# An adaLN transformer block: the work ahead of the batch loop cut in column chunks and spread over the first batches

## The chip, the cores and the metric

The kernel runs on one core of a Trainium2 chip. The metric is the device time of one launch in microseconds (us), the median of several runs. A core has five engines that run their own instruction streams and meet at semaphores: TensorE (PE, matrix products), VectorE (DVE), ScalarE (ACT), GpSimd (POOL) and SyncE (SP, which here only issues DMA transfers).

## What is computed

For 32 batches of 256 rows by 128 channels:

```python
mod = (silu(c) @ wmod).reshape(32, 6, 1, 128)      # sa, ca, ga, sb, cb, gb
ga, gb = sign(g) * max(|g|, 0.25)                  # both gates
h = layernorm(x) * (1 + ca) + sa
x = x + ga * attention(h, Wq, Wkv, Wo, bo)         # 16 heads of 64, strictly later keys masked
h = layernorm(x) * (1 + cb) + sb
x = x + gb * ffn(h)                                # fp4 block quantiser (blocks of 16) on each input
                                                   # and on w_gate, w_up, w_down; silu(gate) * up
```

All of it is float32. The softmax takes its maximum over all 256 keys and masks afterwards.

## The kernel before

**The loop.** One turn `i` handles batch `i`'s attention, batch `i-1`'s output projection, residual and second layer norm, and batch `i-2`'s feed-forward part, and it prepares batch `i+1` (layer norm, transposed and modulated input). A turn has four stages `j` (PAIRS), each with two units `2j` and `2j+1`; a unit is a pair of heads. `iterations` writes out the turns -1, 0, 1, 2, runs 3 to 30 as a hardware loop, and writes out the last ones. The table `SHARED` is the order, by hand, of what PE writes to the three shared PSUM banks `ps_m` in each stage ("t" transposes of probabilities, "qk" and "v" projections, "xt" the next batch's transposed input, and so on); "qk" of stage `j` serves the units of stage `j+1`.

**How units flow.** PE writes the scores of both units to `ps_s` (`scores`, L922), DVE reduces them to row maxima (`maxima`, L736), PE adds the mask on the diagonal blocks (`mask`, L931), ACT takes exponentials and their sums (`exponentials`, L563), DVE makes reciprocals (`denominators`, L742 and L745), POOL multiplies (`normalize`, L435 and L437), PE transposes (L806), DVE or ACT copies to `probs_t`, PE multiplies with the values (`values`, L949).

**Float32 by parts.** The projections split each float32 operand into a high part (rounded to fp32r) and the rest: ACT writes `wq_r[0]`, `wkv_r[0]` (L512 to L516), DVE subtracts for `wq_r[1]`, `wkv_r[1]` (L611, L617). A product is three matmuls (`matmul_parts`). The transposed input is split in the same way: ACT writes `h_t` and `h_r[0]` (L545), DVE writes `h_r[1]` (L755, with two inputs in SBUF).

**Ahead of turn 0.** SP issues all loads from its one queue, in this order: cond, w_mod, w_q whole, the key half of w_kv, batch 0's x, the value half of w_kv, b_o, w_o, the six pieces of w_gate and w_up, w_down (L370 to L382). ACT makes `tanh` of cond, then the high parts of the three weights of 1024 columns, each as it lands. DVE makes `c_act`, copies `c_t`, writes the low parts of the three weights and `mod_t` (scale and shift of layer norm 1, transposed for all batches) between them; PE transposes `c_act` (L806), multiplies the modulation rows of all batches (L814, two products of 384 columns into `ps_s`) and the two transposed ones (L817). Only then DVE's turn -1 begins: layer norm of batch 0 (`layer_norm_stats` L717, POOL's `rstd` L443 and L445, `normalized` L711), PE's transposes into `ps_m`, ACT's L545, DVE's L755, PE's first two "qk". At the end of turn -1 DVE runs `modulation_rows` (13 steps on 32 x 128 rows, L629 to L641: gates, 1 + cb and so on), which SP stores to `mod_rows` in DRAM for the broadcast loads `mod_a` and `mod_b`, and `weight_scales` (four memsets, L54, L55, L56 of the weight quantiser over 1120 columns). `quantize_magic` of the weights (L62, L65, L66) comes at the end of turn 0, stage 0. POOL runs the three rounding steps (L73, L75, L77) in turn 0, stages 1, 2 and 3. PE transposes the quantised weights in turn 1 at the places `WEIGHT_PLACES` = (0,7), (1,3), (1,4), which later turns use for the feed-forward part; gate of batch 0, at (0,7) of turn 2, is the first to need them.

## Time and profile before

| | before |
|---|---|
| median of 3 runs | 1324.75 us |
| lowest, highest | 1322.56, 1326.55 us |
| the profiled execution: time, span | 1323.2, 1321.3 us |
| busy share PE, DVE, ACT, POOL | 96%, 82%, 63%, 64% |
| mean granted TensorE clock | 0.988 |
| DMA queues, share of 16 engines | 7.0% |

The span is what the profiler saw, from the first instruction to the last; 1.9 us of the run's time lie around it. The busy shares are means over the whole span, so they say little about the opening; for that the windows, the chain and the timeline are read.

### The profile page before, as it was taken

What the parts mean: (1) busy time and instruction counts of PE and PEld (TensorE: products, weight loads), DVE (VectorE), ACT (ScalarE), POOL (GpSimd) and SP (SyncE); (2) the same over time, 40 slices, a digit from 0 to 9 for tenths busy, and PEclk for the clock granted to TensorE, in tenths of its full rate; (3) what the DMA queues carried; (4) which work ended last, traced back from release to release, by engine and by line L of the source; (5) the groups of instructions that cost most, each with busy time, mean ns of one, the idle gap of its engine ahead of it and who ended that gap; (6) DMA issues with size and microseconds to landing.
All of it is one profiled execution on the core that took longest, in us unless ns stands there. A gap on an engine that the chain in (4) does not pass through costs nothing.

```text
span 1321.3 us, 34181 instructions
## 1 busy us (share of the span) xinstructions
PE 1270.0 (96%) x10194; PEld 1033.1 (78%) x10194; DVE 1089.7 (82%) x2565; ACT 837.1 (63%) x2885; POOL 841.2 (64%) x1582
## 2 busy tenths in 40 slices
PE   4999999999999999999999999999999999999984
PEld 3678888788888788888788888888888878888863
DVE  5678888888888888888888888888888888888775
ACT  3666657667667666666766666766666766666640
POOL 1656666766666766666666666676666676666664
PEclk9999999999999999999999999999999999999995
DMA  3000000000000000000000000000000000000000
GB/s 103 18 19 18 12 22 18 22 22 16 12 20 18 22 22 16 20 12 20 20 22 20 17 10 22 18 22 22 16 11 21 18 22 22 16 22 6 19 19 10
DMA packets 38056, 26.53 MB, mean 20 GB/s; under 512 B 2800, under 2 KB 33392, under 8 KB 38032
## 3 DMA queue, kind: packets, MB, share of 16 engines
q1 hardware_dynamic: 38032, 26.23, 7.0%
q8 instruction: 13, 0.21, 0.1%
q14 instruction: 11, 0.09, 0.0%
HBM read 21.94 MB, written 4.28 MB: 20 GB/s over the span
## 4 chain that ended last, share of the span: by engine, by line
PE 92%; DVE 4%; ACT 2%; issue 1%; DMA 1%; POOL 1%; SPq 0%; DVEq 0%; POOLq 0%; ACTq 0%
PE ps_m L827 27%; PE ps_s L922 18%; PE ps_m L806 16%; PE ps_o L949 14%; PE ps_m L873 9%; PE ps_s L931 5%; PE ps_m L897 4%; ACT probs L563 1%; DMA wkv<-L_attn_Wkv 1%; DVE neg_max L736 1%; DVE probs_t L662 0%; DVE qy L62 0%; ACT qk L531 0%; DVE amax L54 0%; DVE qm L66 0%
## 5 line engine op out<-in xcount | busy, mean ns | idle before, releaser
L563 ACT ACTIVATE probs<-ps_s,neg_max 128x128 f32<-128x128 f32 (+1 forms) x1024 | 424.4, 429 | 396.0 <-PE ps_s L931 396.0
L437 POOL TENSOR_SCALAR probs<-probs,r_den 128x256 f32<-128x256 f32 (+1 forms) x768 | 347.6, 468 | 0.0
L736 DVE TENSOR_REDUCE neg_max<-ps_s 128x4 f32<-128x1024 f32 x256 | 303.9, 1218 | 2.5 <-PE ps_s L922 2.3
L922 PE MATMUL ps_s<-qk 64*128 64x256 f32 x2048 | 259.1, 392 | 0.8 <-ACT qk L531 0.8
L662 DVE COPY probs_t<-ps_m 128x512 f32<-128x512 f32 x256 | 176.4, 689 | 80.2 <-PE ps_m L806 76.2
L806 PE MATMUL ps_m<-ident,probs 128*128 128x128 f32 x1536 | 230.9, 273 | 2.4 <-POOL probs L437 1.0
L435 POOL TENSOR_TENSOR probs<-probs,r_den 128x128 f32<-128x128 f32 x256 | 102.1, 399 | 202.5 <-DVE r_den L745 183.8
L922 PEld LDWEIGHTS ps_s<-qk 64*128 64x128 f32 x2048 | 185.3, 187 | 48.3 <-issue 12.3
L563 ACT ACTIVATION_READ_ACCUMULATOR probs<-ps_s,neg_max 128x1 f32 x1024 | 217.7, 213 | 0.0
L73 POOL TENSOR_TENSOR qy<-qy,qm 128x352 f32<-128x352 f32 (+1 forms) x96 | 82.9, 864 | 181.7 <-DVE qm L66 179.4
L949 PE MATMUL ps_o<-probs_t,v 128*64 128x256 f32 (+1 forms) x2048 | 194.7, 332 | 1.5 <-ACT o_t L555 1.5
L949 PEld LDWEIGHTS ps_o<-probs_t,v 128*64 128x64 f32 x2048 | 127.3, 136 | 80.3 <-issue 43.7
L806 PEld LDWEIGHTS ps_m<-ident,probs 128*128 128x128 f32 x1536 | 179.4, 141 | 8.0 <-DVE probs_t L662 2.1
L827 PE MATMUL ps_m<-h_r,wq_r 128*128 128x256 f32 x768 | 156.1, 312 | 2.8 <-DVE h_r L755 2.3
L531 ACT COPY qk<-ps_m 128x512 f32<-128x512 f32 x256 | 153.5, 600 | 3.3 <-PE ps_m L827 3.3
L827 PE MATMUL ps_m<-h_r,wkv_r 128*128 128x256 f32 x768 | 134.1, 283 | 0.0
L873 PE MATMUL ps_m<-wo,o_t 128*128 128x128 f32 x1024 | 121.8, 277 | 0.0
L827 PE MATMUL ps_m<-wkv_r,h_r 128*128 128x512 f32 x384 | 119.0, 418 | 1.4 <-ACT qk L531 1.2
L873 PEld LDWEIGHTS ps_m<-wo,o_t 128*128 128x128 f32 x1024 | 116.8, 192 | 2.9
L827 PEld LDWEIGHTS ps_m<-h_r,wq_r 128*128 128x128 f32 x768 | 108.2, 191 | 11.2 <-DVE h_r L755 2.0
L827 PEld LDWEIGHTS ps_m<-h_r,wkv_r 128*128 128x128 f32 x768 | 110.4, 190 | 0.0
L931 PE MATMUL ps_s<-later_b,ident_b 128*128 128x256 bf16 x512 | 100.9, 279 | 4.0 <-DVE neg_max L736 3.9
(107 smaller groups left out, 1794.2 us busy)
## 6 DMA issues: line engine op xcount, KB each, us to landing
mod_a<-mod_rows SPq DMA_DIRECT2D x32, 256.0 KB, 3.3
x_in<-L_attn_x SPq DMA_DIRECT2D x32, 128.0 KB, 2.1
x_res<-L_attn_x SPq DMA_DIRECT2D x32, 128.0 KB, 2.1
out<-y_out SPq DMA_DIRECT2D x32, 128.0 KB, 1.8
mod_b<-mod_rows SPq DMA_DIRECT2D x32, 64.0 KB, 2.9
wkv<-L_attn_Wkv SPq DMA_DIRECT2D x2, 512.0 KB, 6.9
wq<-L_attn_Wq SPq DMA_DIRECT2D x1, 512.0 KB, 4.1
wo<-L_attn_Wo SPq DMA_DIRECT2D x1, 512.0 KB, 8.2
```

The source lines that it names most:

```text
L435: nc.gpsimd.tensor_tensor(cols, cols, r_den[:, u % 4, 0:1].to_broadcast([P, P]), ALU.mult)
L437: ins = nc.gpsimd.tensor_scalar(cols, cols, r_den[:, u % 4, s:s + 1], 1.0, ALU.mult, ALU.mult)
L531: nc.scalar.copy(qk[:, k % 4, :, :], ps_m[bank][:, :].rearrange("p (n j) -> p n j", n=2)).then_inc(qk_ready, 1)
L563: ins = nc.scalar.activation(probs[:, u % 4, h, t * P:(1 + 2 * t) * P], ps_s[:, 2 * (u % 2) + h, t * N:t * N + (1 + t) * P], ACT.Exp, bias ...
L662: nc.vector.tensor_copy(probs_t[:, 4 * (k % 3):4 * (k % 3) + 4, :], ps_m[bank][:, :].rearrange("p (c j) -> p c j", c=4)).then_inc(pt_ready ...
L736: nc.vector.tensor_reduce(neg_max[:, u % 4, :], ps_s[:, 2 * (u % 2):2 * (u % 2) + 2, :].rearrange("p b (t j) -> p (b t) j", t=2), AX.X, AL ...
L806: return nc.tensor.transpose(dst, src, ident[0:n, 0:n])
L827: mm = nc.tensor.matmul(dst, left[l], right[r], start=(n == 0), stop=(n == 2))
L873: mm = nc.tensor.matmul(ps_m[bank][:, 0:P], o_t[:, u, k * P:(k + 1) * P], wo[:, u, :], start=(u == 0), stop=(u == UNITS - 1))
L922: mm = nc.tensor.matmul(ps_s[:, 2 * (u % 2) + h, t * N:(t + 1) * N], qk[rows, u % 4, 0, t * P:(t + 1) * P], qk[rows, u % 4, 1, :], start=( ...
L931: nc.tensor.matmul(diagonals, ident_b[:, :], later_b[:, :].unsqueeze(1).to_broadcast([P, 2, P]), start=False, stop=True, skip_group_check= ...
L949: mm = nc.tensor.matmul(ps_o[h * DH:(h + 1) * DH, k * N + q0:(k + 1) * N], v[:, keys, col:col + DH], probs_t[:, chunk + 2 * n:chunk + 2 + ...
```

## The change

The body of a turn keeps its order on each engine (it is now written out call by call, with the same sequence); what changes is ahead of turn 0 and in turns 0 and 1. Turn -1 is gone, its work stands ahead of the loop.

- **Loads.** ACT's queue takes batch 0's x and the first 256 columns of w_q. SP's queue takes the rest: w_q and the key half in chunks of 256, 256 and 512 columns, the value half in two of 512, w_mod in one of 256 and one of 512 columns, w_o last of the weights. Batch 1's x is loaded by SP behind all of them.
- **Opening.** DVE clears its padding and normalises batch 0 first. PE makes only the two transposed modulation products before the transposes of batch 0. Only the first chunk's high and low parts lie ahead of the first "qk". Chunk 1 and the first value half follow ahead of turn 0; low parts of chunk 2 and of the second value half are in DVE's turn 0, stage 0; ACT makes their high parts ahead of turn 0.
- **Modulation rows.** PE makes one product of 384 columns in turn 0, stage 0 and one in stage 1, after the scores, into `ps_o`. ACT copies them as its first step of those stages. The 13 steps of row arithmetic run on POOL: 6 before `normalize(0)` of stage 0, 7 in stage 1. SP stores the rows in stage 3 instead of stage 1.
- **Weight quantiser.** DVE takes the maxima at the end of turn 0's stage 0, scales and quotients at the end of stage 1, the two magic steps at the end of stage 2. POOL rounds in turn 0 stage 3, turn 1 stage 0 and turn 1 stage 1. PE's places are (1,7), (2,4), (3,3) of turn 1.

```diff
-        WEIGHT_PLACES = [(0, 7), (1, 3), (1, 4)]
+        WEIGHT_PLACES = [(1, 7), (2, 4), (3, 3)]
+        QK_CHUNKS = (slice(0, 2 * P), slice(2 * P, 4 * P), slice(4 * P, INNER))
+        V_CHUNKS = (slice(INNER, INNER + HALF), slice(INNER + HALF, 2 * INNER))
 # SP
-            sp.dma_start(w_mod_s[:, :], w_mod).then_inc(cond_in, 16)
-            sp.dma_start(wq[:, :], w_q).then_inc(wq_in, 16)
-            sp.dma_start(wkv[:, 0:INNER], w_kv[:, 0:INNER]).then_inc(wk_in, 16)
-            sp.dma_start(x_in[:, :, :], x_v[0]).then_inc(x_loaded, 16)
-            sp.dma_start(wkv[:, INNER:2 * INNER], w_kv[:, INNER:2 * INNER]).then_inc(wv_in, 16)
+            sp.dma_start(w_mod_s[:, 0:2 * P], w_mod[:, 0:2 * P]).then_inc(wmod_in[0], 16)
+            sp.dma_start(wkv[:, QK_CHUNKS[0]], w_kv[:, QK_CHUNKS[0]]).then_inc(wk_in[0], 16)
+            sp.dma_start(wq[:, QK_CHUNKS[1]], w_q[:, QK_CHUNKS[1]]).then_inc(wq_in[1], 16)
+            sp.dma_start(wkv[:, QK_CHUNKS[1]], w_kv[:, QK_CHUNKS[1]]).then_inc(wk_in[1], 16)
+            sp.dma_start(wkv[:, V_CHUNKS[0]], w_kv[:, V_CHUNKS[0]]).then_inc(wv_in[0], 16)
+            sp.dma_start(w_mod_s[:, 2 * P:6 * P], w_mod[:, 2 * P:6 * P]).then_inc(wmod_in[1], 16)
+            sp.dma_start(wq[:, QK_CHUNKS[2]], w_q[:, QK_CHUNKS[2]]).then_inc(wq_in[2], 16)
+            sp.dma_start(wkv[:, QK_CHUNKS[2]], w_kv[:, QK_CHUNKS[2]]).then_inc(wk_in[2], 16)
+            sp.dma_start(wkv[:, V_CHUNKS[1]], w_kv[:, V_CHUNKS[1]]).then_inc(wv_in[1], 16)
...
-                    if i_is(i, 0) and j == 1:
-                        sp.wait_ge(setup_dve, SETUP_ROWS)
+                    if i_is(i, 0) and j == 3:
+                        sp.wait_ge(rows_steps, ROWS_STEPS)
                         sp.dma_start(mod_rows, rows[:, :, :]).then_inc(rows_out, 16)
 # POOL
+            def attention_rows():
+                step = Steps(pool, rows_steps)
+                pool.wait_ge(mod_copied, 1)
+                gate_row(step, 2, 0, 0)
+                pool.wait_ge(bo_in, 16)
+                step(nc.gpsimd.tensor_tensor(rows[:, 1, :], rows[:, 0, :], bo_rows[:, :], ALU.mult))
...
+                    if j == 0:
+                        normalize(i, -1)
+                        if i_is(i, 0):
+                            attention_rows()
+                        if i_is(i, 1):
+                            round_weights(1)
+                        normalize(i, 0)
+                        keep()
+                    elif j == 1:
+                        normalize(i, 1)
+                        if i_is(i, 0):
+                            ffn_rows()
+                        if i_is(i, 1):
+                            round_weights(2)
+                        residual()
+                        input_rstd()
+                        round_hidden(i - 2, 0)
+                        normalize(i, 2)
...
+                    elif j == 3:
+                        normalize(i, 5)
+                        if i_is(i, 0):
+                            round_weights(0)
+                        round_hidden(i - 2, 1)
+                        normalize(i, 6)
+                        round_ffn_in()
+            rstd(0, ln1_pool, ln1_steps, LN_STEPS, mv1, var1, rstd1)
             iterations(pool, body)
 # ACT
-            act.wait_ge(cond_in, 32)
+            act.dma_start(x_in[:, :, :], x_v[0]).then_inc(x_loaded, 16)
+            act.dma_start(wq[:, QK_CHUNKS[0]], w_q[:, QK_CHUNKS[0]]).then_inc(wq_in[0], 16)
+            act.wait_ge(cond_in, 16)
             nc.scalar.activation(c_act[:, :], c_in[:, :], ACT.Tanh, scale=0.5).then_inc(setup_act, 1)
...
+                    if i_is(i, 0) and j < 2:
+                        modulation_copy(j)
...
+            high_parts(0)
+            act.wait_ge(setup_dve, SETUP_MODT)
+            shared = shared_steps(-1)
+            shared_reads(shared, 2, 8)
+            high_parts(1)
+            value_high_part(0)
+            shared_reads(shared, 3, 1)
+            shared_reads(shared, 3, 6)
+            high_parts(2)
+            value_high_part(1)
             iterations(act, body)
 # DVE
+                        maxima(0)
+                        maxima(1)
+                        if i_is(i, 0):
+                            low_parts(2)
...
+                    if i_is(i, 0) and j == 0:
+                        value_low_part(1)
+                        weight_maxima()
+                    if i_is(i, 0) and j == 1:
                         weight_scales()
+                        weight_quotients()
+                    if i_is(i, 0) and j == 2:
+                        weight_exponents()
+                        weight_magic()
...
+            step = Steps(dve, setup_dve)
+            dve.wait_ge(x_loaded, 16)
+            layer_norm_stats(x_in, stats1, mv1, ln1_steps, 0)
+            dve.wait_ge(setup_act, 1)
+            step(nc.vector.scalar_tensor_tensor(c_act[:, :], c_act[:, :], 1.0, c_in[:, :], ALU.add, ALU.mult))
+            step(nc.vector.tensor_scalar(c_act[:, :], c_act[:, :], 0.5, None, ALU.mult))
+            dve.wait_ge(ln1_pool, 2)
+            normalized([xn[:, t, :] for t in range(2)], x_in, mv1, rstd1, xn_ready)
+            dve.wait_ge(setup_pe, 1)
+            step(nc.vector.tensor_copy(c_t[:, :], ps_o[:, 0:B]))
+            dve.wait_ge(setup_pe, 2)
+            step(nc.vector.tensor_copy(mod_t[:, 0, :], ps_o[:, 0:B]))
+            step(nc.vector.tensor_scalar(mod_t[:, 1, :], ps_o[:, B:2 * B], 1.0, None, ALU.add))
+            low_parts(0)
+            dve.wait_ge(ht_ready, 2)
+            nc.vector.tensor_tensor(h_r[1][:, :], h_t[:, :], h_r[0][:, :], ALU.subtract).then_inc(hr_ready, 1)
+            low_parts(1)
+            value_low_part(0)
             iterations(dve, body)
 # PE
+                    if i_is(b, 0) and k in (0, 2, 4):
+                        pe.wait_ge(attn_high, k + 2)
+                        pe.wait_ge(qk_low, k + 2)
...
                     if has.attn:
                         scores(2 * j)
                         scores(2 * j + 1)
+                    if i_is(i, 0) and j < 2:
+                        modulation_matmul(j)
...
+            shared = shared_steps(-1)
+            for place in ((2, 8), (3, 1), (3, 6)):
+                shared_step(*shared[place][0:4])
             iterations(pe, body)
```

## Rows read from the trace of the kernel before

**Rows 1.** Page part 4: shares of the chain that ended last, by engine.
```profile
PE 92%; DVE 4%; ACT 2%; issue 1%; DMA 1%; POOL 1%; SPq 0%; DVEq 0%; POOLq 0%; ACTq 0%
```
**Rows 2.** Windows: stretch, us, busy PE, PEld, DVE, ACT, POOL, clock, DMA, GB/s.
```profile
60.03:97.71 37.68, 36.38 (x298) 28.79 (x296) 26.26 (x63) 24.26 (x86) 17.86 (x38) 1.00 0.06 17
97.71:136.82 39.11, 39.07 (x320) 32.04 (x319) 33.23 (x80) 25.95 (x90) 26.17 (x50) 1.00 0.07 18
126.27:1225.30 1099.03, 1094.38 (x8906) 895.48 (x8904) 936.76 (x2212) 727.56 (x2522) 728.21 (x1372) 1.00 0.07 18
```
**Rows 3.** Chain in order of time, 0 to 62 us: start us, us, what.
```profile
3.07 7.35 DMA wkv<-L_attn_Wkv
...
12.87 0.48 DVE stats L717 x2
...
15.58 0.68 PE ps_m L806 x2
...
17.82 0.47 DVE mod_r L629
...
26.26 0.61 PE ps_s L931 x2
```
**Rows 4.** Timeline of the opening: start us, us, engine line op tiles [idle before].
```profile
0.73 1.28 ACT L509 ACT_TABLE_LOAD   x1 [0.73 <-PEq L983]
...
6.09 2.77 PE L814 MATMUL ps_s<-w_mod_s,c_t 128*32 128x384 f32 x4 [0.36 <-DVE c_t L606]
...
8.79 1.06 PE L817 MATMUL ps_m<-c_t,w_mod_s 128*128 128x32 f32 x4
...
17.39 0.42 DVE L755 TENSOR_TENSOR h_r<-h_t,h_r 128x256 fp32r<-128x256 f32 x1 [1.96 <-ACT h_r L545]
...
17.87 1.01 PE L827 MATMUL ps_m<-h_r,wq_r 128*128 128x256 f32 x3 [1.64 <-DVE h_r L755]
...
20.73 2.69 PE L922 MATMUL ps_s<-qk 64*128 64x256 f32 x16
...
26.70 0.37 ACT L563 ACTIVATE probs<-ps_s,neg_max 128x128 f32<-128x128 f32 x1 [5.28 <-PE ps_s L931]
```
**Rows 5.** Page part 6: DMA issues, KB each, median us from issue to landing.
```profile
x_in<-L_attn_x SPq DMA_DIRECT2D x32, 128.0 KB, 2.1
```
**Rows 6.** Window of PE alone (stretch, us, busy, clock, DMA, GB/s).
```profile
26.00:27.00 1.00, 0.74 (x4) 0.50 0.00 0
```
**Rows 7.** Timeline of PE: the same three matmuls before and after 29 us.
```profile
27.31 0.84 PE L827 MATMUL ps_m<-h_r,wkv_r 128*128 128x256 f32 x3
...
29.73 0.52 PE L827 MATMUL ps_m<-h_r,wkv_r 128*128 128x256 f32 x3
```
**Rows 8.** Page part 5 (busy, mean ns, idle before): a POOL product of 128 columns.
```profile
L435 POOL TENSOR_TENSOR probs<-probs,r_den 128x128 f32<-128x128 f32 x256 | 102.1, 399 | 202.5 <-DVE r_den L745 183.8
```
**Rows 9.** Timeline: POOL's smallest arithmetic step.
```profile
13.80 0.19 POOL L443 TENSOR_TENSOR var<-mv,ln_eps 128x2 f32<-128x2 f32 x1 [10.96 <-DVE mv L721]
```
**Rows 10.** Timeline: POOL normalising beside DVE's weight quotients, and later without them.
```profile
29.28 2.82 POOL L437 TENSOR_SCALAR probs<-probs,r_den 128x256 f32<-128x256 f32 x3
...
29.40 1.53 DVE L62 SCALAR_TENSOR_TENSOR qy_w<-wf,inv_w 128x1120 f32<-128x1120 f32 x1
...
33.58 1.28 POOL L437 TENSOR_SCALAR probs<-probs,r_den 128x256 f32<-128x256 f32 x3
```
**Rows 11.** Timeline of turn 0, stage 2: maxima and the mask behind them.
```profile
40.31 2.55 DVE L736 TENSOR_REDUCE neg_max<-ps_s 128x4 f32<-128x1024 f32 x2
...
42.97 0.11 PEld L931 LDWEIGHTS ps_s<-later_b,ident_b 128*128 128x128 bf16 x2 [0.17 <-DVE neg_max L736]
```
**Rows 12.** Timeline of turn 0, stage 3: a weight rounding step and its neighbours.
```profile
50.72 2.10 POOL L77 TENSOR_TENSOR wfq<-qy_w,scale_w 128x1120 f32<-128x1120 f32 x1
51.00 2.10 DVE L755 TENSOR_TENSOR h_r<-h_t,h_r 128x256 fp32r<-128x256 f32 x1 [0.23 <-ACT h_r L545]
...
53.24 0.59 PE L827 MATMUL ps_m<-h_r,wq_r 128*128 128x256 f32 x3 [0.67 <-DVE h_r L755]
```

More of the change, by code:

```diff
@@ L567, in exponentials @@
                         ins.then_inc(exp_done, 1)
-                    if has.attn:
-                        exponentials(2 * j, 0)
-                        exponentials(2 * j, 1)
-                    first = 5 if j == 2 else 4
-                    for n in range(first):
-                        shared_reads(n)
-                    if has.attn:
-                        exponentials(2 * j + 1, 0)
-                    for n in range(first, 6):
-                        shared_reads(n)
-                    if j == 1 and has.prev:
-                        out_copy()
```

543 lines of the change are left out of this document (354 added, 189 removed).

## The prediction

> **What bounds the kernel now.** I read the chain of the whole span first: 92% of it is PE, 4% DVE, 1% DMA [rows 1]. Then the windows, to see whether that holds everywhere. Turn 2 takes 39.11 us with PE busy for 39.07; the 28 turns of the hardware loop take 1099.03 us, 39.25 each, with PE busy for 1094.38 [rows 2]. So from turn 2 on PE has no hole, and nothing in the change touches these turns: each engine's calls stand in the same order. Turn 1 has a hole of 1.3 us (37.68 less 36.38) [rows 2]. What is left is the opening. There the chain runs over the last weight transfer (it lands at 10.42), the layer norm at 12.87, the transposes of batch 0 at 15.58, then over DVE from 17.82 on (modulation rows and weight scales, one step after the other) before the maxima, and reaches the first mask only at 26.26 [rows 3]. ACT waited 5.28 us for that mask and started its first exponential at 26.70 [rows 4]. Since PE is dense afterwards, a microsecond by which the first mask comes earlier is a microsecond of the kernel, unless a later stage of turns 0 or 1 gives it back. The sum is therefore the shift of one point, the first exponential, less what turns 0 and 1 lose, plus what they gain.
>
> **Part 1, to batch 0's normalised input.** x is now the first transfer of ACT's queue. A lone transfer of its size lands 2.1 us after issue [rows 5]; issued at about 0.75, with others beside it, I take 3.1 for its landing. ACT's two issues push its 1.28 us table load [rows 4] back by about 0.9, so the tanh can start at 2.95. It used to wait for w_mod until 4.4. From the start of the layer norm to the transposes the trace has 15.58 - 12.87 = 2.71 us [rows 3]; the two c_act steps fit in the time in which DVE waits for POOL's rstd. So xn is done at about 5.7. DVE then copies c_t (5.9), PE makes the two modulation products (0.25 to start, 1.06 busy [rows 4]) until 7.2, and the transposes of batch 0, queued behind them, begin at 7.25.
>
> **Part 2, to the first projection and the first mask.** From the transposes to the first projection it took 17.87 - 15.58 = 2.29 us [rows 3, 4]. The low parts of chunk 0 (two steps of 256 columns) lie in that stretch, while ACT makes h. The first projection is then at 9.55, instead of 17.87: 8.3 us earlier. The two projections and the scores of both units took PE from 17.87 to 20.73 + 2.69 = 23.42 [rows 4], 5.55 us, which gives 15.1. One modulation product is new behind them: four records of L814 are spread over 2.77 us, so one product is 1.28 us at that clock [rows 4]. ACT copies it (0.55, as DVE's copy of the same rows took) before its first exponential. The maxima are done by then (about 15.0 and 16.3), since DVE has nothing of the 7 us of steps left in front of them. First mask at 16.4, first exponential at 17.05 against 26.70 [rows 4]. **Shift: 9.65 us.** The high parts of chunk 1 and of a value half (about 1.2 us of ACT) lie before the first copy of qk at 11.2; those of chunk 2 and the last half (1.7 us) end near 14.7. Both are covered, if the slices have landed.
>
> **Part 3, turn 0, stage 0.** The six POOL steps of the attention rows have 32 x 128 operands, which the trace doesn't show on POOL. Bounds are the 0.19 of a step of two columns and the 0.40 of one of 128 columns and 128 partitions [rows 8, 9]; nearer to the latter, I take 0.33. They end at 19.1, when the first reciprocals are due: nothing, or 0.4 at the upper bound, on POOL alone. The low parts of chunk 2, half a value part and the weight maxima add 3.2 us to DVE, but the quotients and the magic steps (3.2 us) leave the same stage. Nothing.
>
> **Part 4, stage 1.** The second modulation product at the full clock is 0.64, ACT's copy 0.55, ahead of the exponentials; PE used to wait 0.5 for the maxima there. I charge 0.45. The seven POOL steps (2.3 us) take the place of the weight rounding of 2.58 in that stage. The end of DVE's stage gets the scales (0.85) and the quotients (1.53 [rows 10]).
>
> **Part 5, stage 2.** The quotients end at about 32.4 on the new clock; the maxima of the stage come after them, at 32.8, where the shifted old time is 40.31 - 9.65 = 30.7 [rows 11]. PE used to reach the mask at 42.97 with 1.4 us between the first maxima's end and its use, so it would now wait 0.9 to 1.2. I charge 0.9; bounds are 0 (POOL's rows at the lower bound) and 2.4 (all of the new DVE work uncovered). The magic steps at the stage's end (1.7) fall in a hole of DVE of 2.4 us. Nothing.
>
> **Part 6, stage 3.** A rounding step on POOL and the subtraction L755 ran together: the latter took 2.10 where it takes 0.42 alone, and PE waited 0.67 for it [rows 4, 12]. Now a longer step of the quantiser (2.58, an addition of 1120 columns) stands at the same place. I charge 0.5 more. The Trainium skill (SBUF — State Buffer, section "Who interferes with whom") says that a DVE instruction with two SBUF inputs contends with a GpSimd instruction that reads SBUF and that the second to issue fully blocks. By that rule the subtraction lasts until the rounding ends, which the trace agrees with (51.00 + 2.10 against 50.72 + 2.10, after a pause); if it were only slowed, the charge would be nothing.
>
> **Part 7, turn 1 and the clock.** The rounding steps in turn 1 fall in pauses of POOL of 3.8 and 3.9 us, with maxima and PSUM copies on DVE beside them; the weight transposes only change places. The hole of 1.3 us in turn 1 bounds the gain from that; I take nothing. The granted clock was 0.50 of full (1.2 GHz) at 26 to 27 [rows 6], after PE had been idle for 2.85 us, and three matmuls took 0.84 instead of 0.52 there [rows 7]. In the new order that pause is filled by the modulation product. About 3.1 us of PE at the low level go; most of it was hidden behind ACT. I take 0.6 as a gain (0 to 1.2).
>
> **Sum.** 9.65 - 0.45 - 0.9 - 0.5 + 0.6 = 8.4 us. On the profiled execution, 1323.2, this gives 1314.8, span 1312.9; that execution lies 1.55 under the median of 1324.75. On the median it is 1316.3, which I forecast.
>
> **Rivals.** *The shift comes through whole.* Stages 1 to 3 have more slack than I see, and the hole of turn 1 closes too: 9.65 + 1.2 + 1.0 is about 11.9, so 1313. For it: PE's waits in turn 0 besides the opening are short and many. Against: DVE is busy in its stages 1 and 2. *The slices come slowly.* ACT and DVE take them in order, so a late slice of w_q or w_kv holds all that is queued behind it, the copies of qk first. In the trace 10.4 us sufficed for 2 MB [rows 3], and the first exponential needs nearly the same 2 MB by 15, so transfers must take half again as long before it starts to count; at 17 to 18 us for the lot the loss is 3 to 4 us and the time 1320. The Trainium skill (DMA: Bandwidth & Descriptors, section "Bandwidth") gives the rule to batch DMAs to 1 MiB or more, and its table has 138 GB/s for 64 KB; an estimate from that page's figure, with all 2.1 MB at that rate, has the last slice at about 17.3. No row here shows transfers of 1 KB rows, so the trace neither agrees nor disagrees. *The loop settles in a worse phase, and the kernel is slower.* The turns are the same code, but turn 0 hands them over with other distances between DVE and POOL. If L755 met a POOL read in each turn as in stage 3 of turn 0, PE would wait 0.67 [rows 12] in each of 28 turns, 18.8 us, and the time would be 1335; it decides from 0.3 us a turn. Against it: PE is busy 1094.38 of 1099.03 us and DVE meets the same order each turn. *The change doesn't do what it says* (the mask still late, because DVE is held by something else) would leave 1322 or more; the waits as written show no such holder.
>
> **How the numbers follow.** Forecast 0.62, shift whole 0.20, slow slices 0.11, no effect 0.04, worse phase 0.03. The forecast's own range is 1314 to 1319 (bounds of parts 5 and 7). To hold 8 in 10 with the spread of the runs, 1322.56 to 1326.55, I take in the rival at 1313 and most of the slow slices: 1312 to 1320.5. A measurement tells about 0.3% from no change, 4 us, so faster means under 1320.8: the first two cases and most of the third, 0.90. Same 0.07, slower 0.03.
>
> **What would show it.** First projection at 9.5, first mask at 16.4, first exponential at 17. In stage 2 of turn 0 PE waits about 1 us for DVE's maxima. L755 in stage 3 takes over 2 us. Batch loop 39.2 us a turn as before. The prediction is wrong if ACT or DVE waits for a DMA after 5 us for more than a microsecond, or if a turn of the loop has another length.

## The result

| | before | after |
|---|---|---|
| median of 6 runs each | 1323.98 us | 1319.20 us |
| lowest to highest | 1322.56 to 1326.55 us | 1317.02 to 1319.81 us |
| profiled execution, its span | 1323.20, 1321.3 us | 1317.02, 1314.9 us |
| mean granted clock there | 0.988 | 0.988 |

The ratio after to before is 0.996, with a 95% interval of 0.9948 to 0.9971: faster by 4.8 us, where the forecast had 8.4 (1316.3 us). A second measurement, below, gave 1317.25 us and 0.9949 (0.9936 to 0.9963). Both lie in the range of 1312 to 1320.5; the first median lies just outside the forecast's own range of 1314 to 1319.

The readings below all use one mark: the time at which PE starts the scores of a stage (L922 before, L1128 after). Since PE is dense from turn 2 on, the distance of this mark between the two kernels is what is won up to there.

| mark | before | after | won |
|---|---|---|---|
| first exponential (ACT) | 26.70 | 15.50 | 11.2 |
| scores of turn 0, stage 1 | 32.38 | 20.35 | 12.0 |
| turn 0, stage 2 | 39.13 | 27.34 | 11.8 |
| turn 0, stage 3 | 48.37 | 38.75 | 9.6 |
| turn 1, stage 0 | 56.19 | 47.11 | 9.1 |
| turn 1, stage 2 | 77.84 | 68.74 | 9.1 |
| turn 1, stage 3 | 86.62 | 78.69 | 7.9 |
| turn 2, stage 0 | 93.86 | 86.64 | 7.2 |
| turn 2, stage 1 | 103.47 | 95.80 | 7.7 |
| last scores | 1262.38 | 1254.72 | 7.7 |
| end of the span | 1321.3 | 1314.9 | 6.4 |

Windows of the kernel after, the same stretches of turn 2 and of the 28 loop turns as in [rows 2] (us, then busy PE, PEld, DVE, ACT, POOL, clock, DMA, GB/s):

```profile
90.02:129.15 39.13, 39.09 (x320) 32.03 (x318) 33.79 (x80) 25.95 (x90) 26.66 (x51) 1.00 0.07 18
118.60:1217.64 1099.04, 1094.18 (x8906) 893.85 (x8905) 937.58 (x2213) 727.63 (x2522) 728.32 (x1372) 1.00 0.06 18
```

To 0.02 us these are the lengths of before. The loop neither gains nor loses, and what moved stands in the opening and the tail. The chain of the whole span says the same (PE 92% still; DVE and DMA less, POOL more than in [rows 1]):

```profile
PE 92%; DVE 3%; POOL 2%; ACT 1%; issue 1%; DMA 0%; DVEq 0%; POOLq 0%
```

The opening of the kernel after (timeline: start us, us, engine, line, tiles, and in brackets how long the engine had waited and for whom), with the lines that answer to [rows 4]:

```profile
1.74 1.28 ACT L591 ACT_TABLE_LOAD   x1 [1.74 <-issue]
...
3.21 0.49 DVE L773 BATCH_NORM_STATS2 stats<-x_in 128x6 f32<-128x128 f32 x2 [1.65 <-DMA x_in<-L_attn_x]
...
9.18 1.01 PE L1029 MATMUL ps_m<-h_r,wq_r 128*128 128x256 f32 x3 [1.63 <-DVE h_r L995]
...
12.04 2.28 PE L1128 MATMUL ps_s<-qk 64*128 64x256 f32 x16
14.26 0.83 PE L1022 MATMUL ps_o<-w_mod_s,c_t 128*32 128x384 f32 x2
15.02 0.39 PE L1138 MATMUL ps_s<-later_b,ident_b 128*128 128x256 bf16 x2
...
15.50 0.35 ACT L659 ACTIVATE probs<-ps_s,neg_max 128x128 f32<-128x128 f32 x1
```

The stretch of 7 us in which DVE worked on modulation rows and weight scales between scores and mask is gone: the mask follows the scores after one product. Then stage 1 to stage 2 of turn 0, where 2.2 us are given back (POOL, DVE and PE in turn):

```profile
23.68 0.28 POOL L480 COPY rows<-mod_r 32x128 f32<-32x128 f32 x1
24.05 0.54 POOL L481 TENSOR_SCALAR rows<-mod_r 32x128 f32<-32x128 f32 x1
24.67 0.64 POOL L464 TENSOR_SCALAR gates<-mod_r 32x128 f32<-32x128 f32 x1
...
27.14 0.45 POOL L468 TENSOR_TENSOR rows<-gates 32x128 f32<-32x128 f32 x1
...
27.94 0.71 POOL L495 TENSOR_TENSOR rstd<-var,expo 128x2 f32<-128x2 f32 x1
...
28.68 0.97 DVE L782 SCALAR_TENSOR_TENSOR xn<-x_in,mv,rstd 128x128 f32<-128x128 f32 x2 [2.41 <-POOL rstd L495]
...
30.42 1.32 DVE L758 SCALAR_TENSOR_TENSOR qy_w<-wf,inv_w 128x1120 f32<-128x1120 f32 x1
...
32.08 2.33 DVE L858 TENSOR_REDUCE neg_max<-ps_s 128x4 f32<-128x1024 f32 x2
...
33.33 0.39 PE L1138 MATMUL ps_s<-later_b,ident_b 128*128 128x256 bf16 x2 [2.08 <-DVE neg_max L858]
```

Read it from below: PE waits 2.08 us for the maxima, these start late because DVE's normalisation and quotients stand before them, and DVE had waited 2.41 us for POOL's rstd, which stands behind seven row steps (23.68 to 27.6). Stage 3 of turn 0, which answers to [rows 12]:

```profile
41.17 2.56 POOL L73 TENSOR_TENSOR qy_w<-qy_w,qm_w 128x1120 f32<-128x1120 f32 x1
...
41.38 2.63 DVE L874 TENSOR_TENSOR h_r<-h_t,h_r 128x256 fp32r<-128x256 f32 x1 [0.23 <-ACT h_r L631]
...
44.16 0.60 PE L1029 MATMUL ps_m<-h_r,wq_r 128*128 128x256 f32 x3 [1.20 <-DVE h_r L874]
```

And stage 2 of turn 1, where the next 1.2 us go:

```profile
75.45 1.01 DVE L782 SCALAR_TENSOR_TENSOR xn<-x,mv,rstd 128x128 f32<-128x128 f32 x2
76.39 0.55 DVE L727 CAST wgu_r<-ps_m 128x384 fp32r<-128x384 f32 x1
...
77.58 0.96 PE L1029 MATMUL ps_m<-wkv_r,h_r 128*128 128x512 f32 x3 [0.89 <-DVE wgu_r L728]
```

### The profile page after: what moved, and what is told of

Same layout as the page of the kernel before. It is cut to its first block, busy times and chain, and to the rows that moved or that the text cites. A ratio compares the mean times of both kernels' runs of the same rounds, so it can differ in the third digit from the quotient of the medians.

```text
span 1314.9 us, 34208 instructions
## 1 busy us (share of the span) xinstructions
PE 1268.4 (96%) x10194; PEld 1031.1 (78%) x10194; DVE 1086.3 (83%) x2557; ACT 838.2 (64%) x2892; POOL 848.3 (65%) x1595
## 4 chain that ended last, share of the span: by engine, by line
PE 92%; DVE 3%; POOL 2%; ACT 1%; issue 1%; DMA 0%; DVEq 0%; POOLq 0%
PE ps_m L1029 27%; PE ps_s L1128 18%; PE ps_m L1003 16%; PE ps_o L1158 14%; PE ps_m L1081 9%; PE ps_s L1138 5%; PE ps_m L1105 4%; ACT probs L659 0%; DVE neg_max L858 0%; DVE probs_t L793 0%; DVE xn L782 0%; POOL probs L451 0%; POOL rstd L495 0%; DVE qy L62 0%; DVE h_r L874 0%
## 5 line engine op out<-in xcount | busy, mean ns | idle before, releaser
L1128 PE MATMUL ps_s<-qk 64*128 64x256 f32 x2048 | 258.5, 391 | 0.6 <-ACT qk L617 0.6
L1128 PEld LDWEIGHTS ps_s<-qk 64*128 64x128 f32 x2048 | 185.1, 186 | 47.8 <-issue 12.4
```

The lines of the kernel that those rows point to most:

```text
L1128: mm = nc.tensor.matmul(ps_s[:, 2 * (u % 2) + h, t * N:(t + 1) * N], qk[rows, u % 4, 0, t * P:(t + 1) * P], qk[rows, u % 4, 1, :], start=( ...
```

## The experiments

My theory after the result (A): the shift of the opening passes whole to the loop, less three losses, each with a queue order behind it; the rest of the distance to the forecast is the tail, where PE's clock differs from one execution to the next. Rival theories (B) are named with each run. "Gain" below is the last scores against the 1254.72 of the kernel after, unless another mark is named.

**rstd_first: POOL's order in stage 1 of turn 0.**

```diff
                         normalize(i, 1)
-                        if i_is(i, 0):
-                            ffn_rows()
...
                         input_rstd()
+                        if i_is(i, 0):
+                            ffn_rows()
```

> Edit: in turn 0, stage 1, POOL makes the next batch's rstd before the seven steps of the feed-forward rows instead of after them. Theory A (the missing 2.1 us of stage 2 are a queue: DVE waits 2.41 us for that rstd, and the weight scales and quotients behind it then run into the maxima): rstd ends near 24.6 instead of 28.65, DVE's quotients end near 29.4 instead of 31.74, the first maxima of stage 2 start near 29.9 instead of 32.08, PE's wait of 2.1 us before the mask of stage 2 goes below 0.3, and that mask comes near 31.3 instead of 33.33. From there on every mark up to the end of the hardware loop is about 2 us earlier. Theory B (the quotients themselves are too long for the stage, as the prediction had it): the wait stays at 0.9 us or more, and the gain is at most 1.2 us.

One execution: 1315.41 us, last scores at 1253.13, gain 1.6. From the scores of stage 2 to those of stage 3 it took 9.25 us (27.91 to 37.16) instead of 11.41. DVE and PE:

```profile
26.76 0.61 DVE L782 SCALAR_TENSOR_TENSOR xn<-x_in,mv,rstd 128x128 f32<-128x128 f32 x2
...
30.02 2.33 DVE L858 TENSOR_REDUCE neg_max<-ps_s 128x4 f32<-128x1024 f32 x2
...
31.75 0.39 PE L1138 MATMUL ps_s<-later_b,ident_b 128*128 128x256 bf16 x2
```

DVE no longer waits for rstd, the maxima start 2 us earlier and the mask follows without a pause. The whole loss of stage 2 was this queue order: with the quotients, which I had blamed, still in front of the maxima, the stage is as long as in the kernel before (9.24 us, 39.13 to 48.37). The edit gives back the full 2.2 us. The gain at the last scores is only 1.6 because this execution had lost 0.6 before the edit acts (stage 2 at 27.91 against 27.34): its first scores took 2.77 us instead of 2.28 (2.00 at the full clock).

**reads_first: DVE's order in stage 2 of turn 1.**

```diff
                         denominators(4)
+                        if i_is(i, 1):
+                            shared_reads(2, 4)
...
                         hidden_magic(i - 2, 1)
-                        if i_is(i, 1):
-                            shared_reads(2, 4)
```

> Edit: in turn 1, stage 2, DVE reads the second transposed weight out of its PSUM bank before it normalises the attended rows (xn2) instead of after. Theory A (the bank is held: PE waits 0.89 us for the read because it is queued behind the normalisation, and this is the larger part of the 1.17 us lost in that stage): the wait before the value projection in turn 1, stage 2 goes, the scores of stage 3 come near 77.7 instead of 78.69, everything after is 0.8 to 1.1 us earlier. Theory B (the third work of DVE in this stage is too much wherever it stands): the wait moves to the modulated input or to the next maxima, and the scores of turn 2 stay within 0.3 us of 86.64.

One execution: last scores at 1253.68, gain 1.0. The scores of stage 3 start at 77.71 instead of 78.69, and PE's wait of 0.89 is gone:

```profile
76.61 0.95 PE L1029 MATMUL ps_m<-wkv_r,h_r 128*128 128x512 f32 x3
```

So the reads of the transposed weights held a PSUM bank that the next projection needs, and the normalisation ahead of them (1.01 us) was the delay. The time of this execution, 1316.98 us, shows nothing of the gain: its tail was 61.2 us long, 1.0 more than that of the kernel after.

**both: the two edits together.**

```diff
+ the edit of rstd_first
+ the edit of reads_first
```

> Edit: the reorderings of rstd_first and reads_first together; nothing is left out. If the two losses are separate queues they add: 2.0 + 1.0 = 3.0 us against the changed kernel up to the end of the hardware loop, so some 10.7 us against the kernel before at that point, and a time of 1313.5 to 1316.5, the rest depending on the clock in the last 50 us. If they hide each other (both only fill the same slack) the gain against the changed kernel is 2 us or less.

1314.29 us (1313.16 to 1314.35), 0.9921 of before (0.9903 to 0.9940). At the scores of turn 2, stage 1 (92.62 against 95.80) the gain is 3.2, the sum of the 2.2 in stage 2 of turn 0 and the 1.0 in stage 2 of turn 1: the two losses are independent. The last scores stand at 1252.06, a gain of 2.7, since from that mark on this execution took 1159.4 us where that of the kernel after took 1158.9, through the same instructions.

**light_round: the clash in stage 3.** POOL's rounding there is cut to one block of 16 columns of 1120.

```diff
-                quantize_round(..., wfq, WB // BLOCK, scale_w, qy_w, qm_w, parts=(part,))
+                blocks = 1 if part == 0 else WB // BLOCK
+                quantize_round(..., wfq, blocks, scale_w, qy_w, qm_w, parts=(part,))
```

> Edit: POOL's first rounding step of the weights (turn 0, stage 3) covers 16 columns instead of 1120, so most of the weights' first rounding is left out; all else stays. Theory A (the two-input subtraction of DVE at line 874 is held until POOL's instruction ends): it takes 0.42 to 0.45 us instead of 2.63, PE's wait of 1.20 us before the next projection goes, and turn 1 starts (scores) 1.2 to 1.7 us earlier than 47.11. Theory B (DVE and POOL only share and slow one another, and PE's wait has another cause): the subtraction stays above 1 us or the wait stays above 0.5.

This kernel leaves out nearly all of the first rounding of the weights. The subtraction took 0.42 us instead of 2.63, and stage 3 took 7.24 us (41.07 to 48.31) instead of 8.36: the clash costs 1.1. The end did not gain (last scores 1255.81), since something else came in before it. PE alone in stage 2, windows (us, busy, clock, DMA, GB/s) and two lines of the timeline:

```profile
33.00:34.00 1.00, 0.00 (x0) 1.00 0.06 18
34.00:35.00 1.00, 0.91 (x7) 0.84 0.72 203
35.00:36.00 1.00, 1.00 (x7) 0.50 1.03 104
```

```profile
34.09 0.39 PE L1139 MATMUL ps_s<-later_b,ident_b 128*128 128x256 bf16 x2 [2.08 <-DVE neg_max L859]
...
35.46 0.84 PE L1030 MATMUL ps_m<-h_r,wkv_r 128*128 128x256 f32 x3
```

After the pause of 2.08 us the granted clock fell to 0.50 (1.2 GHz) until about 38, and three products took 0.84 instead of 0.52; stage 2 took 12.97 instead of 11.41 us. The kernel after had the same pause of 2.08 us, and its clock stayed at 1.00. So one execution with such a pause lost 1.6 us behind it and another nothing. That is one source of scatter.

**late_norm: the shift itself.** Slices and spread work stay as in the change, but batch 0 is normalised behind all parts of the weights again.

```diff
             high_parts(0)
+            high_parts(1)
+            high_parts(2)
+            value_high_part(0)
+            value_high_part(1)
             act.wait_ge(setup_dve, SETUP_MODT)
             shared = shared_steps(-1)
             shared_reads(shared, 2, 8)
-            high_parts(1)
-            value_high_part(0)
...
-            dve.wait_ge(x_loaded, 16)
-            layer_norm_stats(x_in, stats1, mv1, ln1_steps, 0)
...
             low_parts(0)
+            low_parts(1)
+            low_parts(2)
+            value_low_part(0)
+            value_low_part(1)
+            dve.wait_ge(x_loaded, 16)
+            layer_norm_stats(x_in, stats1, mv1, ln1_steps, 0)
```

> Edit: the changed kernel with batch 0's layer norm put back behind all weight parts: ACT makes all high parts before the transposed input, DVE all low parts before the layer norm; slices, modulation rows and quantiser stay as changed. This splits the early shift (11.2 us at the first exponential) into the order of the opening and the spreading of row and quantiser work. Theory A (the order of the opening is worth most of it, since the last slice lands near 11 us): the layer norm starts near 12.2 instead of 3.2, the first projection comes at 16.5 to 17.5 instead of 9.18, the first exponential at 22.5 to 24, so 3 to 4 us are left from the spreading alone, and the time is 1323 to 1326, about that of the kernel before. Theory B (the spreading is what counts, the order little): first exponential before 20.

One execution: 1328.22 us, beside a median of 1325.35 (1323.00 to 1326.46) of before. Two lines of its timeline:

```profile
12.47 0.48 DVE L773 BATCH_NORM_STATS2 stats<-x_in 128x6 f32<-128x128 f32 x2
...
17.40 1.01 PE L1025 MATMUL ps_m<-h_r,wq_r 128*128 128x256 f32 x3 [1.63 <-DVE h_r L993]
```

The first projection stands at 17.40, near the 17.87 of before, the first exponential at 25.06 against 26.70, and the last scores at 1265.90, 3.5 later than in before. Theory A had put the first exponential at 22.5 to 24 and the time at 1323 to 1326; both came later. Of the 11.2 us the early layer norm brings 8.2 at the first projection (17.40 to 9.18) and 9.6 at the first exponential (25.06 to 15.50); the 1.4 between are the clock, for the first scores took 3.63 us here and 2.28 in the kernel after. The rest of the change alone brings 1.6 there and then loses 5.2 in turns 0 and 1. About 1.6 of that is another stretch at 1.2 GHz (30.4 to 33.8, in stage 1, behind a pause of PE of 1.69 us in stage 0). Without it the last scores would still stand some 1.9 us behind those of before: in this one execution the rest of the change, without the early layer norm, gains nothing.

**whole_loads: the slices.** x still comes first, but each weight half is one transfer; ACT and DVE still work in chunks.

```diff
-            sp.dma_start(wkv[:, QK_CHUNKS[0]], w_kv[:, QK_CHUNKS[0]]).then_inc(wk_in[0], 16)
-            (eight more slices of w_q, w_kv and w_mod)
+            sp.dma_start(w_mod_s[:, :], w_mod).then_inc(wmod_in[0], 16)
+            sp.dma_start(wkv[:, 0:INNER], w_kv[:, 0:INNER]).then_inc(wk_in[0], 16)
+            sp.dma_start(wkv[:, INNER:2 * INNER], w_kv[:, INNER:2 * INNER]).then_inc(wv_in[0], 16)
...
-            act.dma_start(wq[:, QK_CHUNKS[0]], w_q[:, QK_CHUNKS[0]]).then_inc(wq_in[0], 16)
+            act.dma_start(wq[:, :], w_q).then_inc(wq_in[0], 16)
```

> Edit: the changed kernel with w_q (on ACT's queue), w_mod, the key half and the value half of w_kv loaded whole, in this order, and everything computed in the same chunks. Theory A (slices are needed so that chunk 0 is there in time): w_q shares the transfers with x, w_mod and the keys, the keys land near 7.5 us, ACT's high parts of chunk 0 end near 8.2 and the transposed input behind them at 9.3 instead of 8.68, the first projection is at 9.8 to 11 instead of 9.18, and the value half near 10.5 delays ACT's first copy of qk by under 1 us: 1 to 2.5 us in all. Theory B (what matters is the order of the engines' work, not how the loads are cut): the first exponential stays within 0.5 us of 15.50.

One execution: 1320.41 us, last scores at 1258.08, 3.4 later than in the kernel after. Timeline:

```profile
9.77 1.01 PE L1023 MATMUL ps_m<-h_r,wq_r 128*128 128x256 f32 x3 [2.08 <-DVE h_r L989]
...
12.63 3.37 PE L1122 MATMUL ps_s<-qk 64*128 64x256 f32 x16
```

Up to the first projection the larger transfers cost 0.6 us (9.77 against 9.18). The rest is the clock, twice: it rose later, so that the first scores took 3.37 us instead of 2.28 (1.1), and it fell to 0.50 behind a pause of 1.69 us in stage 0, so that stage 1 took 8.63 instead of 6.99 (1.6). The sum is 3.3. How much of the latter two comes from the edit, and how much from this execution, one execution can't tell: warm_again, below, has both with the slices as they were.

**warm_tail: the clock of the tail.** In the last two turns PE gets 60 useless products of 512 columns into a PSUM bank that nobody reads.

```diff
+            BUSY = {(0, 0, 2): 3, (0, 0, 7): 2, (0, 2, 4): 3, (0, 3, 3): 2, (0, 3, 5): 20, (0, 3, 7): 2,
+                    (1, 0, 7): 3, (1, 1, 7): 4, (1, 2, 4): 14, (1, 3, 3): 2, (1, 3, 5): 3, (1, 3, 7): 2}
...
+                def keep_busy(n):
+                    for _ in range(n):
+                        nc.tensor.matmul(ps_s[:, 0, :]..., ident_b[:, :], later_b[:, :]..., start=True, stop=True)
...
+                    if i_is(i, B) and (j, n) == (0, 2):
+                        pe.wait_ge(exp_done, 16 * B)
+                    if isinstance(i, int):
+                        keep_busy(BUSY.get((i - B, j, n), 0))
```

> Edit: the changed kernel with 60 products of 512 columns without use, in the last two turns, put ahead of the steps for which PE waits there (20 before the transposes that wait 5.6 us, 14 before those that wait 4.0); they write a PSUM bank that nobody reads any more. Theory A (the scatter of the runs from 1317.0 to 1319.8 us, and 1.4 us of the missing gain in the profiled run, are PE at its lower clock in the last 50 us): the granted clock stays 1.00 until the end, the last 60 us shrink from 60.2 to 55 to 57, the runs agree within 1 us, and the median is 1313.5 to 1316. Theory B (the end is a chain of DVE and POOL steps, the clock there costs nothing): no change, or slower by up to 3 us where the products are in the way.

1314.09 us (1313.37 to 1315.98), 0.9923 of before (0.9909 to 0.9937). The loop ends as before the edit (last scores at 1254.65), the tail is 56.4 us instead of 60.2. Windows of the kernel after, then of this one (all engines, columns as above):

```profile
1264.00:1274.00 10.00, 6.83 (x50) 4.89 (x51) 4.08 (x10) 1.60 (x4) 5.28 (x10) 0.91 0.07 20
1274.00:1284.00 10.00, 7.30 (x50) 6.53 (x50) 6.73 (x21) 1.42 (x3) 3.46 (x5) 0.92 0.01 2
1284.00:1294.00 10.00, 3.40 (x14) 2.19 (x12) 6.88 (x16) 0.48 (x1) 6.60 (x10) 0.59 0.00 0
1294.00:1304.00 10.00, 4.59 (x12) 3.26 (x12) 6.38 (x15) 0.93 (x2) 2.48 (x4) 0.50 0.07 20
```
```profile
1284.00:1294.00 10.00, 6.73 (x36) 3.72 (x34) 6.13 (x14) 0.64 (x2) 6.45 (x9) 1.00 0.06 18
1294.00:1304.00 10.00, 7.39 (x37) 3.76 (x36) 7.44 (x16) 1.24 (x3) 3.43 (x4) 1.00 0.01 2
```

PE is filled instead of idle and keeps 1.00 (2.4 GHz); the chain of small products at the end then runs through 3.7 us sooner. The runs do not lie closer together, though (2.6 us apart, where theory A had 1).

**before_warm, warm_again, after_again: how much of the median is the tail.** The same 60 products in the kernel before (the diff is that of warm_tail), warm_tail once more, and the kernel after once more with nothing changed.

```diff
 (kernel before)
+ the edit of warm_tail
```

> Edit: the kernel before, with the same 60 products without use in its last two turns as in warm_tail. Theory A (the end costs both kernels the same 3.7 us of PE at the lower clock, give or take its chance of one more drop): the median is 1319 to 1322 and the runs lie closer together than those of the kernel before; against warm_again in the same runs the difference is the shift at the end of the hardware loop, 7.0 to 8.5 us, so the change is worth what the two traces show there and the end only blurs it. Theory B (the change itself makes the end slower): before_warm is only 4 to 6 us above warm_again.

```diff
 (kernel after)
+ the edit of warm_tail
```

> Edit: none against warm_tail, the changed kernel with the 60 products, run again beside before_warm on the same chip. Theory A: 1313 to 1316, 7.0 to 8.5 us under before_warm. Theory B: 4 to 6 us under it.

```diff
 (kernel after, no edit)
```

> Edit: none, the changed kernel in the same runs as the others of this call. Its granted clock is to be read run by run: with the clock as the cause of the scatter the runs at 0.988 lie 2 to 2.5 us under those at 0.986 or lower, in both kernels, and the median is 1316.5 to 1319.5.

| | median | lowest to highest | ratio to before (95%) |
|---|---|---|---|
| before_warm | 1322.59 | 1321.18 to 1325.31 | 0.9984 (0.9975 to 0.9993) |
| warm_again | 1316.25 | 1313.16 to 1317.82 | 0.9928 (0.9914 to 0.9942) |
| after_again | 1317.25 | 1316.14 to 1319.34 | 0.9949 (0.9936 to 0.9963) |

With the tail warm in both, the change is worth 6.3 us in this pair and 8.5 if warm_tail is taken instead of its twin (1322.59 less 1314.09). The 8.5 sets two separate measurements against each other. The expectations were 7.0 to 8.5 for A and 4 to 6 for B: the pair lies between the two, and identical code differs by 2.2 us from one measurement to the other. The median of before_warm missed its 1319 to 1322, and its runs are as far apart as those of before. The blur lies ahead of the tail. The windows of PE in the two profiled executions show the clock's part (before_warm, then warm_again):

```profile
30.00:35.00 5.00, 4.31 (x16) 0.50 0.01 2
```
```profile
22.00:23.00 1.00, 1.00 (x8) 0.50 0.00 0
```

before_warm's last scores stand at 1265.77, 3.4 behind those of before, though no instruction in front of them is changed. Only a part of that is the clock. Its first projection already came at 19.36 instead of 17.87, 1.5 later, because the key half of w_kv landed later and held ACT's high part, which stands at 8.60 in before:

```profile
9.96 1.04 ACT L514 CAST wkv_r<-wkv 128x1024 fp32r<-128x1024 f32 x1 [3.26 <-DMA wkv<-L_attn_Wkv]
```

From there to the scores of turn 2, stage 1 (105.97 against 103.47) another 1.0 goes, with more time at the lower clock. The last 0.9 goes in the loop: from that mark to the last scores it took 1159.8 us against 1158.9, with the clock at 1.00. The profiled executions of after_again and warm_again took 1159.8 too, the first ones of before and after and that of best_open 1158.9; no run shows why. The kernel after, in all of its profiled variants that keep the sliced loads and the order of the opening, had its first projection between 9.17 and 9.42, so that late landing did not recur there. warm_again lost 1.6 in stage 1. after_again says more. Its five executions order themselves by the mean clock: 0.988 or 0.989 took 1316.14, 1317.03 and 1317.25, and 0.986 took 1319.25 and 1319.34. The six of the first measurement fall into the same two groups (two at 0.988 with 1317.02 and 1317.40, four at 0.986 with 1319.01 to 1319.81). Windows of 10 us each from the last scores on were read for PE alone; the second and third are shown, of after_again (tail 58.7 us) and of reads_first (tail 61.2 us), whose instructions there are the same:

```profile
1265.39:1275.39 10.00, 6.54 (x53) 1.00 0.07 20
1275.39:1285.39 10.00, 5.74 (x44) 1.00 0.01 2
```
```profile
1263.68:1273.68 10.00, 7.05 (x48) 0.75 0.07 20
1273.68:1283.68 10.00, 7.30 (x48) 0.90 0.01 2
```

The clock falls earlier or later in the first 30 us of the tail, and since the instructions are the same, that is the difference of 2.5 us between the two tails. The executions of before don't order themselves so plainly (1324.34 at 0.984, 1326.31 at 0.986): they have pauses of PE in the opening as well, and before_warm shows a load that can land late.

**best: all that was learnt, together.** both and warm_tail, and POOL's rounding in stage 3 waits until the subtraction L874 is through.

```diff
+ the edits of both and warm_tail
...
                         if i_is(i, 0):
+                            pool.wait_ge(hr_ready, 2)
                             round_weights(0)
```

> Edit: the changed kernel with rstd_first, reads_first and warm_tail together, and in turn 0, stage 3, POOL waits for the low part of the transposed input before its first rounding step, so that the two no longer meet. Expected if the terms add: 2.0 and 1.0 (as measured together: 2.7 at the last scores), 1.1 for the meeting in stage 3 (DVE's subtraction 0.42 to 0.45 instead of 2.63), 3 to 5 for the clock at the end: 1309 to 1312. If the wait only moves the clash to the following stage (POOL's rounding then holds the reciprocals of unit 6), the 1.1 are missing.

1310.15 us (1309.53 to 1312.00), 0.9893 of before (0.9878 to 0.9909). Stage 3 took 7.25 us (37.23 to 44.48) instead of 8.36, as in light_round but with all of the rounding done. The timeline of the two, to be held against the pair of the kernel after:

```profile
39.86 0.43 DVE L875 TENSOR_TENSOR h_r<-h_t,h_r 128x256 fp32r<-128x256 f32 x1 [0.22 <-ACT h_r L632]
...
40.37 2.57 POOL L73 TENSOR_TENSOR qy_w<-qy_w,qm_w 128x1120 f32<-128x1120 f32 x1 [0.69 <-DVE h_r L875]
```

The subtraction takes 0.43 alone and 2.63 beside the rounding; delaying the rounding by 0.69 us costs PE nothing (stage 0 of turn 1 takes 9.60 us in both).

**best_open: the clock of the opening too.** 15 more useless products, 8 before the first projection and 7 in PE's pause of 1.7 us in stage 0.

```diff
             pe.wait_ge(pool_setup, POOL_SETUP)
+            opening_busy(3, ps_s[:, 0, :])
...
+            opening_busy(2, ps_s[:, 0, :])
             pe.wait_ge(setup_dve, SETUP_CT)
...
+                    if i_is(i, 0) and (j, n) == (0, 8):
+                        pe.wait_ge(mod_copied, 1)
+                        opening_busy(7, ps_o[:, :])
...
+                if place == (3, 1):
+                    opening_busy(3, ps_s[:, 0, :])
```

> Edit: best (all three reorderings and the 60 products at the end) with 15 more products without use in the opening: 3 before PE's first transpose, 2 after it, 3 before the first projection, 7 in turn 0, stage 0, where PE waits 1.7 us for ACT's copy of qk. Theory A (the first projections and scores run at 1.2 GHz only because PE was idle before): the first projection's three matmuls take 0.52 to 0.6 instead of 1.01 or 0.84, the scores of stage 1 come at 19 to 19.8 instead of 20.3 to 21.0, the median is 1308 to 1310 and the runs agree within 1 us. Theory B (8 products at the low clock are too little, or they are in the way): the scores of stage 1 stay at 20.3 or later and the time is 1310 or more.

1309.70 us (1308.58 to 1310.56), 0.9884 of before (0.9869 to 0.9900). Timeline:

```profile
9.18 1.01 PE L1040 MATMUL ps_m<-h_r,wq_r 128*128 128x256 f32 x3 [0.36 <-DVE h_r L996]
9.98 0.67 PE L1040 MATMUL ps_m<-h_r,wkv_r 128*128 128x256 f32 x3
10.49 0.52 PE L1040 MATMUL ps_m<-h_r,wq_r 128*128 128x256 f32 x3
...
11.33 2.00 PE L1151 MATMUL ps_s<-qk 64*128 64x256 f32 x16
```

The clock is up at about 10.3 us instead of 12.7, where the products turn shorter; the scores start at 11.33 instead of 12.04, those of stage 1 at 19.35 instead of 20.35, and the last ones at 1249.45, 1.75 before those of best. Some 0.7 of these 1.75 is that best's own opening was slow (stage 1 at 21.01). But the tail of this profiled execution was 58.1 us where best's was 56.5, its clock having fallen (0.83 in one window of 10 us) in spite of the fillers. The intervals of best and best_open overlap: the gain of the opening is shown in the marks, not in the median. It is the fastest version run, 15 us under the kernel before (1324.74) and 7.6 under after_again (1317.25), which were measured beside it.

## Why the prediction was right, and where it was off

The mechanism held: a microsecond won at the first mask is one at the end unless turns 0 or 1 give it back, and the loop is untouched [rows 2]. The terms, from the marks above:

| term | forecast | measured |
|---|---|---|
| shift of the first exponential | 9.65 | 11.2 |
| clock in stage 0 | +0.6 | +0.8 |
| stage 1 | -0.45 | -0.2 |
| stage 2 | -0.9 | -2.2 |
| stage 3 | -0.5 | -0.5 |
| turn 1 | 0 | -1.4 |
| loop | 0 | 0 |
| tail | 0 | -1.3 |
| sum, on the profiled executions | 8.4 | 6.4 |

*Parts 1 and 2, the shift, were too small by 1.5.* The first projection came at 9.18, not 9.55 (stats at 3.21, as put). From there to the end of the scores it took 5.1 us instead of 5.55, and the new modulation product 0.76 instead of 1.28. The products took 2.86 us in both kernels; the difference is the scores, 2.28 against 2.69, in which the clock rose earlier than in the row that I had used [rows 4]. The modulation product I had taken from a row at the low clock, and it ran at the full one. ACT's copy and the exponential took 0.17 less than put. The slices were in time: ACT and DVE waited for no DMA after 5 us. whole_loads, with fewer and larger transfers, had its first projection 0.6 us later. The rule of the Trainium skill (DMA: Bandwidth & Descriptors, section "Bandwidth") that I had weighed, to batch to 1 MiB or more, is one for bandwidth. No run here has a transfer of 1 MiB; between slices of 128 to 256 KB and loads of 384 and 512 KB, the slices were the faster at this start, where what counts is when the first part is there. late_norm shows that the early layer norm alone is 8.2 of the 11.2, or 9.6 with the clock that rises sooner for it.

*Part 3, stage 0 at nothing, held*, though two of POOL's steps took 1.07 and 1.09 and not 0.33. POOL had the room.

*Part 4 was near.* PE's wait before the maxima went with the work in front of them.

*Part 5 is the first step that failed.* I charged 0.9 for quotients in front of the maxima. The pause of PE was 2.08 and the loss 2.2, near the outer bound of 2.4, and through another door: seven row steps took 3.9 us (23.68 to 27.6) instead of 2.3, and POOL's rstd of the next batch is queued behind them. The size came from a row of 128 columns on 128 partitions (0.40, [rows 8]) and one of two columns ([rows 9]), and I had taken 0.33; most steps took 0.45 to 0.64, above my upper bound. And I had asked what the maxima wait for on DVE, but not who waits for POOL behind the rows. rstd_first moves that one call and gets all of it back. There the quotients still make the maxima start 0.9 later within the stage than in before (2.1 against 1.2 us after the scores), and it costs nothing: the 1.4 us of slack that I had counted cover it.

*Part 6 was right in mechanism and about right in size.* The subtraction took 2.63 and ended with the rounding (41.38 + 2.63 = 44.01, 41.17 + 2.56 = 43.73; in [rows 12] 53.10 and 52.82). best, where the two don't meet, shows that the whole clash costs 1.1, of which the kernel before already paid about half with its own rounding step. That the second of the two is fully blocked, as the Trainium skill has it (SBUF — State Buffer, section "Who interferes with whom"), agrees with these ends, both 0.28 us behind the rounding's, though not to the last tenth: alone the subtraction takes 0.42.

*Part 7 is the second step that failed.* "The weight transposes only change places" was true for PE and wrong for DVE, where their reads stand behind a normalisation and hold a PSUM bank: 1.2 us in stage 2 of turn 1, of which reads_first gets 1.0 back, and 0.7 in stage 3, where PE waits 0.43 for the copy of another transposed weight. 0.45 comes back in stage 0 of turn 2. The 0.7 was not tried by itself. The clock's 0.6 in stage 0 was right in kind and measured 0.8: the second unit's mask follows the first's after 0.95 us (15.02 to 15.97) instead of 1.69 (26.26 to 27.95), with the same products between them.

*The tail was not in the sum.* Nothing in it is changed, and yet it was 58.9 us in before and 60.2 in after, with the clock at 0.91 and 0.92 in two windows (shown with warm_tail) where before had 1.00, in these windows of its own:

```profile
1270.00:1280.00 10.00, 6.05 (x49) 4.37 (x49) 5.76 (x15) 3.29 (x9) 7.05 (x13) 1.00 0.08 20
1280.00:1290.00 10.00, 7.29 (x61) 6.38 (x57) 6.54 (x21) 1.42 (x3) 3.19 (x5) 1.00 0.01 2
```

That is PE's clock in one execution, as reads_first and after_again show. The last step from 6.4 us in the profiled executions to 4.8 in the medians is of the same kind: the profiled execution of after is its fastest, 2.2 under its median, while that of before lies 0.8 under its own. What the change is worth with equal clocks in both tails is about 7.7 by the marks of this pair and 7.2 by the last scores of before_warm and warm_again (1265.77 and 1258.54); the warmed medians give 6.3 and 8.5 and so don't settle it to better than 2 us.

*That the sum came out near was in part luck.* The shift, its clock and stage 1 were together 2.0 better than forecast, and stage 2, turn 1 and the tail 4.0 worse; the two errors cancelled by half.

Of the rivals, the slow slices and the slower loop phase did not occur, the second with a loop turn of 39.25 us in both. "The shift comes through whole" was half right: the shift was larger than forecast, but nearly half of what was won by stage 1 (5.6 of 12.0 us) was given back in turns 0 and 1 and in the tail.

## What to carry to other kernels

When work is moved off a critical wait into "gaps", look at what is queued behind it on its new engine, and let the small step that others wait for (here rstd, the PSUM reads) go first: two such swaps were worth 3.2 us at turn 2, where the large change had brought 7.7. Size small POOL steps by a row of the same kind and as many columns: fewer partitions did not make them cheaper here. And when PE has pauses in the opening or the tail, compare marks of equal place before comparing medians, since the clock there moved the end by 1.6 and 2.5 us. Filling the tail's pauses with useless products shortened the tail by 3.7 us, but it didn't end the scatter: the runs lay 2.6 and 4.7 us apart (warm_tail, warm_again), those of the kernel after 2.8 and 3.2.

## What the runs showed of the hardware that I had not expected

- A pause of PE of 1.7 to 2.1 us was followed, in the same or the next stage, by a stretch of 3 to 4 us at 1.2 GHz in four profiled executions, at a cost of 1.6 us each (light_round, late_norm, whole_loads, warm_again), and in others, the kernel after among them, by none.
- Both kernels run their last 30 us at 1.2 GHz (0.50 to 0.60 granted). Useless products kept 1.00 and saved 3.7 us, though they gave PE more to do.
- POOL's steps on 32 partitions x 128 columns were no cheaper than that on 128 x 128: 0.45 for two tensors, 0.52 to 0.64 for a tensor and scalars, against 0.40 [rows 8]. In two cases beside DVE's two-input steps of 512 columns they took 1.07 and 1.09.
- The same load of 512 KB, issued from the same place in the same code, held ACT until 8.60 us in one profiled execution of the kernel before and until 9.96 in another (before_warm), which moved the first projection by 1.5 us.
